# A GNN kernel on one core: GpSimd's indirect transfers of the first edge stage, issued two scatters and two gathers at a time

## The reference

```
mi  = concat(x[src_bi], x[tgt_bi], edge_feats_bi)        # both directions of every edge
h   = relu(layernorm(mi @ msg_w1 + msg_b1)) @ msg_w2 + msg_b2
agg = segment_sum(h, tgt_bi, num_segments=3125)
upd = relu(layernorm(concat(x, agg) @ upd_w1 + upd_b1)) @ upd_w2 + upd_b2
out = x + upd
```

## Time and profile before

| | |
|---|---|
| Median of 3 runs | 5482.18 us (5475.38 to 5486.58) |
| The profiled execution | 5478.13 us, its span 5476.4 us |
| Busy share of the span | PE 85%, DVE 84%, POOL 74%, ACT 66% |
| TensorE clock granted, mean | 0.913 |
| Chain that ended last, by engine | POOL 51%, issue 22%, PE 11%, DVE 7%, DMA 5%, ACT 2% |
| Scatters, L1387 | 680, 1125.2 us busy, mean 1655 ns |
| Gathers of the first edge stage, L1405 | 784, 798.4 us busy, mean 1018 ns |

### The profile page before, as it was taken

One profiled execution on the slowest core, in us unless ns is written; L12 is line 12 of the kernel. 1 busy time (PEld: TensorE's weight loads), 2 busy tenths in 40 slices (PEclk: granted clock), 3 DMA queues, 4 the chain that ended last, 5 costly groups with the idle time before them and its releaser, 6 DMA issues.

```text
span 5476.4 us, 94645 instructions
## 1 busy us (share of the span) xinstructions
PE 4669.4 (85%) x27053; PEld 3393.2 (62%) x27130; DVE 4594.6 (84%) x13379; ACT 3624.6 (66%) x12258; POOL 4073.3 (74%) x3715
## 2 busy tenths in 40 slices
PE   3899999999999999985888888588888886999995
PEld 2787777777777777774555555355555554555553
DVE  4899999999999999985888889677887877777776
ACT  3777777777777777762777777376777763555553
POOL 4788888888888888884777777577777764777776
PEclk6889999999989999997999999699999998999997
DMA  8767777777666666653676777466666662555553
GB/s 233 154 161 176 180 177 177 179 177 177 160 157 158 159 153 162 153 114 92 186 206 196 199 197 201 135 209 212 212 210 212 211 188 80 159 159 159 157 160 109
DMA packets 652763, 938.46 MB, mean 171 GB/s; under 512 B 105208, under 2 KB 362354, under 8 KB 651970
## 3 DMA queue, kind: packets, MB, share of 16 engines
q1 hardware_dynamic: 432546, 583.92, 34.7%
q0 software_dynamic: 219680, 348.31, 30.6%
HBM read 616.90 MB, written 318.36 MB: 171 GB/s over the span
## 4 chain that ended last, share of the span: by engine, by line
POOL 51%; issue 22%; PE 11%; DVE 7%; DMA 5%; ACT 2%; SPq 1%; POOLq 0%; DVEq 0%; ACTq 0%
POOL arena L1754 26%; POOL tab L1387 13%; POOL arena L1405 12%; PE PS L1941 2%; DMA arena<-T,srcI 2%; DMA tab<-arena 2%; PE PS L2280 2%; PE PS L1716 1%; PE PS L2258 1%; PE PS L2574 1%; PE PS L317 1%; POOL arena L1436 0%; PE PS L2270 0%; DVE arena L2314 0%; SPq L915 0%
## 5 line engine op out<-in xcount | busy, mean ns | idle before, releaser
L1754 POOL DMA_INDIRECT arena<-T,srcI x2112 | 2017.4, 955 | 801.0 <-issue 627.5
L1387 POOL DMA_INDIRECT tab<-arena x680 | 1125.2, 1655 | 233.6 <-issue 207.8
L1405 POOL DMA_INDIRECT arena<-T,srcI x784 | 798.4, 1018 | 287.2 <-issue 283.5
L1741 DVE TENSOR_TENSOR_SCAN arena<-arena,PS 128x512 f32<-128x512 bf16 x588 | 748.0, 1272 | 175.4 <-PE PS L2592 80.8
L1725 ACT ACTIVATE arena<-PS 128x512 f32<-128x512 f32 x588 | 348.3, 592 | 625.7 <-PE PS L1716 625.6
L1821 DVE TENSOR_SCALAR arena<-PS,nodeid 128x512 bf16<-128x512 f32 x908 | 626.9, 737 | 75.3 <-PE PS L1802 75.3
L1001 PE MATMUL PS<-We,arena 65*128 65x256 f32 x1568 | 497.7, 400 | 74.1 <-DVE arena L1061 53.8
L2574 PE MATMUL PS<-arena 128*128 128x512 bf16 x2323 | 548.5, 383 | 4.2 <-issue 0.2
L1941 PE MATMUL PS<-arena 128*128 128x396 bf16 x2800 | 538.5, 349 | 8.7 <-DVE arena L1821 7.3
L797 PE MATMUL PS<-arena 128*128 128x448 bf16 x2184 | 523.3, 397 | 0.8 <-DVE arena L810 0.8
L1003 PE MATMUL PS<-arena 128*128 128x256 f32 x1568 | 488.0, 393 | 0.0
(11 more groups left out here) (321 smaller groups left out, 10943.1 us busy)
## 6 DMA issues: line engine op xcount, KB each, us to landing
H<-arena SPq DMA_DIRECT2D x784, 256.0 KB, 2.5
arena<-keepR SPq DMA_DIRECT2D x294, 256.0 KB, 4.6
arena<-wF SPq DMA_DIRECT2D x98, 512.0 KB, 5.5
arena<-T,srcI POOLq DMA_INDIRECT x2896, 3.0
arena<-in_ea64T SPq DMA_DIRECT2D x98, 256.0 KB
arena<-sH SPq DMA_DIRECT2D x98, 256.0 KB, 4.6
arena<-dH SPq DMA_DIRECT2D x98, 256.0 KB
arena<-S SPq DMA_DIRECT2D x98, 256.0 KB
```

Source lines behind the costliest of these rows:

```text
L1387: e.indirect_dma_start(out=tabs[k % KT], out_offset=at_rows(iA[b % 10][:, c:c + 1]), in_=X2[n % 3][:, c, :], in_offset=None, compute_op=AL ...
L1405: e.indirect_dma_start(out=Gs[b % NR][:, c, :], out_offset=None, in_=T0, in_offset=at_rows(srcI[:, CB * b + c:CB * b + c + 1])).then_inc(g ...
L1741: ins = e.tensor_tensor_scan(s[b % n][:, h, :], kR[g % 6][:, h0:h0 + CB * P], src[h], s[(b - 1) % n][:, h, CB * P - 1:CB * P] if b else in ...
L1754: e.indirect_dma_start(out=dst[:, c, :], out_offset=None, in_=T_tab, in_offset=at_rows(srcI[:, CB * b + c:CB * b + c + 1])).then_inc(gs.of ...
```

## The change

In the iterations with both kinds, POOL issues scatter 0, scatter 1, gather 0, gather 1, scatter 2, scatter 3, gather 2, gather 3, in place of scatter and gather in turn. The instructions, their operands and their semaphores are the same, and their number too.

```diff
@@ -1420,11 +1420,13 @@
                         e.wait_ge(st_zero.of(0), st_zero.at(KT - 1))
                     if 0 <= i - 1 < NBAT:
                         pool_outside(e, i - 1, some)
-                    for c in range(CB):
+                    for c0 in range(0, CB, 2):
                         if i - 9 in pk.turn_of:
-                            pool_scatter(e, i - 9, c)
+                            pool_scatter(e, i - 9, c0)
+                            pool_scatter(e, i - 9, c0 + 1)
                         if i < NBAT:
-                            pool_gather(e, i, c)
+                            pool_gather(e, i, c0)
+                            pool_gather(e, i, c0 + 1)
                     if 1 <= i <= 6:
                         pool_sub(e, 4 * (i - 1), 4 * i + (i == 6))
                 for k in range(CB * len(pk.by_pool) - KT, CB * len(pk.by_pool)):
```

## The result

| | before | after |
|---|---|---|
| Median | 5478.51 us (5 runs, 5462.27 to 5486.58) | 5507.11 us (5 runs, 5501.52 to 5514.76) |
| Ratio | | 1.0055, 95% interval 1.0045 to 1.0066 |
| Profiled execution | 5478.13 us, span 5476.4 | 5501.52 us, span 5499.8 |

The change made the kernel slower by 29 us by the medians and by 23.4 us between the two profiled executions. The forecast was 16 us less.

What follows compares the result with a forecast made beforehand. POOL's full program was taken to bound the kernel; 0.04 + 0.02 - 0.01 = 0.05 us a group, times 322, saves 16 us: 5478.1 to 5462, or by the median 5482 to 5466; range 5447 to 5486 us.

Steps and rivals of the forecast that it cites:

- What bounds the kernel: In the stage with scatters, POOL's program has no room: 498 of 500 us between 500 and 1000 us.
- What the others have in hand: In the scatter stage the other engines could run about 0.8 us an iteration faster, so POOL's saving up to that counts.
- The number of groups: 161 iterations with both kinds, each with two groups of two scatters and two gathers: 322 groups.
- the waits of others: ACT's copy waits for a scatter landing about 1.3 us earlier; DVE takes gathered batches three iterations later; nobody is short.
- A gather behind a gather: In each group, the gather following a gather issues in 0.95 us, not 0.99: gain 0.04 us each.
- A scatter behind a scatter: In each group, the scatter following a scatter issues in 1.56 us, not 1.58: gain 0.02 us, from nothing to 0.037.
- The price of a longer run: Switching kind behind a longer run seems dearer; for runs of two it charged 0.01 us a group.
- The milder form of the slower rival: Dear switches cost in full 0.18 us a group, up to 58 us, perhaps half for runs of two; slower rival's chance 0.08.
- Waits on the tables: A group's second scatter has 8.2 us, formerly 9.5, before its table's earlier scatter must land; under 2 us in all.
- Long issues stay: Issue time above the medians in the body, 71 us in all, stays; it may change by a fifth, 14 us either way.

Runs made afterwards that it cites:

- e_blocks_plain: Kernel before with four orders in successive iterations (in turn, pairs, four and four, runs of eight) and scatters that don't add; 5386.81 us, one run.
- e_run4: Kernel before with POOL's order changed to four scatters, then four gathers; 5480.90 us against 5473.48, ratio 1.0013.
- e_again: The changed kernel itself, measured once more for a second trace; 6159.71 us against 6136.89 for the kernel before, ratio 1.0030.
- e_t4: Kernel before, scatter and gather still in turn, with four tables in place of three; 5491.21 us against 5476.40, ratio 1.0028.
- e_best: Kernel before with four tables, in turn up to iteration 19, then runs of eight (four scatters, four gathers, turned round every other iteration); 5482.31 us against 5476.40.

## Why the prediction was wrong

*What bounds the kernel* was right. POOL's row is full in both traces, and all of its 24 us came out at the end of the stage. *What the others have in hand,* 0.8 us an iteration, was read too high from the first 23 iterations: in `e_blocks_plain` it is about 0.5. That is still more than the forecast needed.

*The number of groups*, 322, was right, and so was it that *the waits of others* would not matter.

*A gather behind a gather, 0.04 us gained each,* failed. It was read from gathers alone in their iteration, where the switch had been from a single scatter: 0.953. Behind two scatters the second gather takes 0.984, so it gains 0.005, and the first one, which I took to stay at 0.989, takes 1.024.

*A scatter behind a scatter, 0.02 us gained,* failed in the same way: 1.583 and not 1.56, behind a first one of 1.610 and not 1.58. The 1.56 of the tail stood behind a scatter that followed a single gather.

*The price of a longer run, charged at 0.01 us,* is the step that failed; the two readings above are the same error, seen in the second issue of each run. The sum went by 1.578 and 1.558 for the scatters and 0.989 and 0.949 for the gathers. Measured are 0.032, 0.025, 0.035 and 0.035 us more, so the price is 0.127 us a group and not 0.01. Less the gain of 0.06, a group costs 0.067 us more and not 0.05 less, and the 322 groups cost 22 us more and not 16 less. The rows were there. The scatter of 1.66 us behind five gathers, the gather of 1.02 behind the tail's scatters and the second one of 0.99 showed the full price, and I took a run of two to be near a run of one. It is as dear as a run of four or five: the scatter is 1.610 behind two gathers and 1.613 behind four in `e_run4`. The 1.66 itself was high: the least of those scatters is 1.598, and their median in `e_again` is 1.611. That VectorE made the difference is not shown.

The milder form of the slower rival, a dear switch at half its run length, had the right sign and the right row, and half of 58 us as its size; measured are 22. It had a small share of 0.08. Why a switch is dear it didn't say, and no run shows it.

*Waits on the tables, under 2 us,* was too small by 4: the one place was known from its 17.71 us, but not worked out. It showed in the waits as well: one of the scatters' waits that stand under "issue" is 4.4 us long, and the prediction took them all for 0.3. Beyond it the 8.2 us of room were enough, as forecast.

*Long issues stay:* right in sum for the change (31 and 33 us), though they moved from scatters (23 us before, 9 after) to gathers (9 and 23), which is why the scatters' mean fell while their median rose.

## What to carry to other kernels

When an engine is full, its program's length is the sum of its issues, and a few hundredths of a microsecond in each decide; before reordering, look up each issue by what stood two and three places ahead of it, not only by its predecessor. A price read from a run of one doesn't hold for a run of two: take the nearest row on the far side too, and ask which of them the new order makes. Here grouping lowered the sum of the medians only in runs of four and eight, and no order that was tried made the kernel faster: long runs shorten the room of whoever waits for the landing of the same kind, and single long issues took the rest.

## What was not expected of the hardware

- A scatter-add of 128 rows takes POOL 1.545 us to issue in a run, the same scatter without adding 0.959, a gather 0.946.
- How long an issue takes goes by the kinds of about three transfers before it: 1.545 to 1.613 us for the scatter-add, 0.946 to 1.024 for the gather. The medians were the same in two executions of one program. What holds this memory is open. Without the addition it is about half as large, and runs of two cost next to nothing (0.006 us a group and not 0.067).
- While one transfer wrote 3200 single elements, scatters landed up to 17.7 us after their start, and POOL waited 3 to 13 us once, in `e_again`, `e_t4` and `e_best` not at all. That this transfer is the cause was not tried.
- Nearly all long issues touch VectorE's four one-hot writes, and the longest last about 1.3 us over the usual; most issues that start under such writes are not held up.
